# K turned by transposing DMAs from its 16-bit halves, and a part of the up weights split one stage later

## What is computed

```python
h = layernorm(xn, ln_g, ln_b)
q = l2norm(heads(h @ Wq)) * q_scale
k = l2norm(heads(h @ Wk)) * k_scale
logits = where(causal, einsum("bhid,bhjd->bhij", q, k) * 10, -1e9)
out = (softmax(logits) @ heads(h @ Wv)) @ Wo
h = layernorm(out, ln_g, ln_b)
gate = softmax(h @ gate_w + gate_b)
hid = gelu(einsum("bsd,edf->bsef", h, w1) + b1)
moe = sum over e of gate[e] * (hid[e] @ w2[e] + b2[e])
ffn = layernorm(moe, ln_g, ln_b)
```

## Time and profile before

| what | value |
|---|---|
| median of 3 runs | 1125.51 us (1121.51 to 1126.7) |
| the profiled execution's own time | 1120.17 us |
| its span, first to last instruction | 1118.4 us |
| mean granted clock of TensorE | 0.986 |
| busy: PE, PEld, DVE, ACT, POOL | 96%, 82%, 86%, 70%, 25% |

### The profile page before, as it was taken

The page is one execution under the profiler, slowest core; times in us unless marked ns, Lnnn a source line. Parts: engine busy times, 40 slices in busy tenths (PEclk is TensorE's granted clock), DMA queues, the critical chain, the costliest instruction groups (busy, mean ns, idle before and its releaser), DMA issues.

```text
span 1118.4 us, 27576 instructions
## 1 busy us (share of the span) xinstructions
PE 1075.0 (96%) x10435; PEld 912.2 (82%) x10435; DVE 959.6 (86%) x2543; ACT 778.9 (70%) x1772; POOL 277.7 (25%) x328
## 2 busy tenths in 40 slices
PE   4877999999999999999999999999999999999997
PEld 1664888888888888888888888888888888888897
DVE  8988798898988989898898989889898888988763
ACT  5873948668595876859677594867759587685653
POOL 2340314224031231404123140412403132140200
PEclk9995999999999999999999999999999999999999
DMA  7010000000000000000000000000000000000000
GB/s 210 7 39 10 2 11 7 1 16 1 11 7 11 6 2 16 1 11 6 6 11 2 11 7 11 6 1 16 2 11 6 11 7 6 6 6 1 7 2 10
DMA packets 18722, 14.60 MB, mean 13 GB/s; under 512 B 2408, under 2 KB 16160, under 8 KB 18592
## 3 DMA queue, kind: packets, MB, share of 16 engines
q1 hardware_dynamic: 17680, 12.76, 3.8%
q10 hardware_dynamic: 912, 0.09, 0.1%
HBM read 10.75 MB, written 2.10 MB: 11 GB/s over the span
## 4 chain that ended last, share of the span: by engine, by line
PE 89%; DVE 4%; issue 3%; ACT 2%; POOL 1%; SPq 0%; DMA 0%; POOLq 0%; DVEq 0%; ACTq 0%
PE O L565 19%; PE O L468 14%; PE S L484 5%; PE U L547 5%; PE U L548 5%; PE U L549 5%; PE J L382 5%; PE S L449 4%; PE J L343 4%; PE U L449 4%; PE S L404 4%; PE J L344 3%; PE J L345 3%; PE S L400 3%; PE O L475 2%
## 5 line engine op out<-in xcount | busy, mean ns | idle before, releaser
L777 ACT ACTIVATE hid<-U,b1c 128x256 f32<-128x256 f32 x512 | 200.5, 474 | 174.8 <-PE U L549 174.7
L565 PE MATMUL O<-w2s,hid 128*128 128x128 f32 x2048 | 251.1, 276 | 0.0
L565 PEld LDWEIGHTS O<-w2s,hid 128*128 128x128 f32 x2048 | 238.6, 192 | 2.9
L928 POOL TENSOR_SCALAR_AFFINE_SELECT P<-P 128x512 f32<-128x512 f32 x128 | 85.0, 664 | 618.6 <-ACT P L750 618.5
L468 PEld LDWEIGHTS O<-Vx,P 128*128 128x128 f32 x1536 | 188.0, 192 | 30.2 <-issue 14.3
L468 PE MATMUL O<-Vx,P 128*128 128x66 f32 x1536 | 188.6, 273 | 3.6 <-POOL P L928 2.0
L1198 DVE TENSOR_TENSOR_SCAN st<-aexp,u 128x256 f32<-128x256 f32 x256 | 178.8, 698 | 0.4 <-issue 0.3
L920 POOL TENSOR_TENSOR raw<-raw,nr 128x512 f32<-128x512 f32 x124 | 132.8, 1097 | 134.9 <-DVE nr L1066 134.9
L1208 DVE SCALAR_TENSOR_TENSOR y<-st,bc,y 128x256 f32<-128x256 f32 x240 | 133.5, 556 | 8.5
L547 PE MATMUL U<-h2h,w1h 128*128 128x256 f16 x480 | 130.9, 273 | 0.0
L549 PE MATMUL U<-h2h,w1l 128*128 128x256 f16 x480 | 130.9, 273 | 0.0
(11 more groups left out here) (204 smaller groups left out, 2048.0 us busy)
## 6 DMA issues: line engine op xcount, KB each, us to landing
xin<-in_L_attn_x SPq DMA_DIRECT2D x16, 128.0 KB, 2.1
xres<-in_L_attn_x SPq DMA_DIRECT2D x16, 128.0 KB, 2.3
hid<-in_L_ffn_w SPq DMA_DIRECT2D x2, 1024.0 KB, 6.5
out_dram<-fin SPq DMA_DIRECT2D x16, 128.0 KB, 1.8
raw<-in_L_ffn_Wq SPq DMA_DIRECT2D x1, 512.0 KB, 4.7
raw<-in_L_ffn_Wk SPq DMA_DIRECT2D x1, 512.0 KB, 6.4
raw<-in_L_ffn_Wv SPq DMA_DIRECT2D x1, 512.0 KB, 7.4
wos<-in_L_ffn_Wo SPq DMA_DIRECT2D x1, 512.0 KB, 11.4
```

Of the source, the lines that this page charges most:

```text
L565: last = mm(O[e % 2][:, t * P:(t + 1) * P], hid[:, e % 2, m, t * P:(t + 1) * P], w2s[:, e * FC + m, :], start=(m == 0), stop=(m == FC - 1))
L777: fn(hid[:, e % 2, f % FC, :], U[q % 2][:, m * SEQ:(m + 1) * SEQ], ACT.Gelu_apprx_tanh, bias=b1c[:, f:f + 1], scale=1.0 / WS).then_inc(gel ...
```

## The change

From the second sequence on K is not turned by TensorE. `high` copies K from `raw` in SBUF to `Kh`, and `low` leaves `Kl`, both in 16 bits and not yet turned. SyncE then turns them with transposing DMAs from `Kh` to `KTh` and from `Kl` to `KTl`, each 128x128: per quarter four for the high half, then four for the low half. That makes 32 per sequence and 480 in all. A quarter's four raise `kt_high[q]` or `kt_low[q]`, which TensorE waits for. Q stays as it was, but its turns now take the two banks by turns. The first sequence is handled as before.

The second part: the low halves of the second half of the up weights are made in four pieces of 512 columns in `body(1)`'s heads' stage, not in one piece in `body(0)`'s experts' stage, and one state of the first scan moves from the heads' stage into that stage.

The core of the diff (left out: the new tiles and semaphores, and the helper that names Q's bank):

```diff
+            def turn_keys(s, quarter, low):
+
+                if quarter == 0 and not low:
+                    sp.wait_ge(st_ready, s * NP)
+                if low:
+                    sp.wait_ge(t_lo, s * NL + 2 * quarter + 2)
+                else:
+                    sp.wait_ge(t_hi, s * NL + 2 * quarter + 2)
+                src, dst, done = ((Kl, KTl, kt_low) if low else (Kh, KTh, kt_high))
+                for p in (2 * quarter, 2 * quarter + 1):
+                    for t in range(T):
+                        sp.dma_start_transpose(dst[:, p, t * P:(t + 1) * P], src[:, t, p * P:(p + 1) * P]
+                                               ).then_inc(done[quarter], 16)
...
                 if older:
                     store_out(i - 2)
+                if new:
+                    for quarter in range(NP // 2):
+                        turn_keys(i + 1, quarter, False)
+                        turn_keys(i + 1, quarter, True)
...
             def scores_for_max(s, p):
 
-                pe.wait_ge(t_hi, s * NL + 2 * (p // 2) + 2)
+                if s == 0:
+                    pe.wait_ge(t_hi, 2 * (p // 2) + 2)
+                else:
+                    pe.wait_ge(t_hi, s * NL + 2 * (p // 2) + 1)
+                    pe.wait_ge(kt_high[p // 2], s * KT)
...
+                if p % 2 == 0 and s > 0:
+                    pe.wait_ge(kt_low[p // 2], s * KT)
...
                     if old and k == 9:
+                        if not older:
+                            pe.wait_ge(w1_low, 2 * W1PARTS)
                         expert_up(i - 1, 0)
                 for m in range(NE + 2):
                     if new and m in TURN_AT:
                         turn_qk(i + 1, TURN_AT[m])
-                        turn_qk(i + 1, TURN_AT[m] + 1)
...
-                    if not old and m == NE + 1:
-                        pe.wait_ge(w1_low, W1PARTS + 1)
...
+                elif s > 0:
+                    half, c0 = quarter // 2, quarter % 2 * 2 * P
+                    act.wait_ge(unit, s * NJ + half * 4 + 4)
+                    from_one(act, kt_high[quarter], (s - 1) * KT)
+                    fn(Kh[:, :, p * P:(p + 2) * P], raw[:, 4 * half + 1:4 * half + 4:2, c0:c0 + 2 * P], ACT.Copy
+                       ).then_inc(t_hi, 1)
...
+                elif s > 0:
+                    half, c0 = quarter // 2, quarter % 2 * 2 * P
+                    from_one(dve, kt_low[quarter], (s - 1) * KT)
+                    V.tensor_tensor(Kl[:, :, p * P:(p + 2) * P], raw[:, 4 * half + 1:4 * half + 4:2, c0:c0 + 2 * P],
+                                    Kh[:, :, p * P:(p + 2) * P], ALU.subtract).then_inc(t_lo, 1)
...
+                    if old and not older and 1 <= k < 1 + W1PARTS:
+                        split_w1(1, k - 1, W1PARTS)
...
-                    if not old and 1 <= m <= 6:
-                        scan(i, m + 9)
-                        add_state(i, m + 9)
+                    if not old and 1 <= m <= 7:
+                        scan(i, m + 8)
+                        add_state(i, m + 8)
...
-                    if not old and m == 3:
-                        split_w1(1, 0, 1)
```

More of the change, by code:

```diff
@@ L38 @@
 KC = 5
+KT = 2 * T * 16
 def build(nc, x, a_log, b, c, dt_w, dt_b, conv_w, conv_b, ln_g, ln_b, Wq, Wk, Wv, q_scale, k_scale,
@@ L114, in build @@
         KTl = sb("KTl", [P, NP, SEQ], F16)
+        Kh = sb("Kh", [P, T, HD], F16)
+        Kl = sb("Kl", [P, T, HD], F16)
         Vx = sb("Vx", [P, T, H, VW])
@@ L200, in build @@
          y_tr, e_vec, e_root, xb_done, xy_done) = (sems[n] for n in names)
+        kt_high = [sem(f"kt_high{q}") for q in range(NP // 2)]
+        kt_low = [sem(f"kt_low{q}") for q in range(NP // 2)]
         def tiles(ap):
@@ L252, in y_bank, with turned, turn_bank @@
             return S2[:, 1, 0:SEQ] if s == LAST else O[0][:, 0:SEQ]
+        def turned(s, n):
+            return n + 1 if s == 0 else NL + (s - 1) * (NP // 2) + n // 2 + 1
+        def turn_bank(s, n):
+            return J[n % 2] if s == 0 else J[n // 2 % 2]
         def step_bank(s):
@@ L372, in turn_qk @@
                 pe.wait_ge(unit, s * NJ + half * 4 + kind * 2 + 2)
-                if n < 2 and s > 0:
-                    pe.wait_ge(v_done, s * 2 * T + 3 + n)
+                if s > 0 and n < 4:
+                    pe.wait_ge(v_done, s * 2 * T + 3 + n // 2)
+                elif s > 0:
+                    pe.wait_ge(t_lo, s * NL + n - 3)
                 elif n < 2:
@@ L718, in high @@
                 quarter, kind = divmod(n, 2)
-                act.wait_ge(t_ready, s * NL + n + 1)
                 p = 2 * quarter
                 if kind == 0:
-                    fn(QTh[:, p, :], J[n % 2][:, 0:SEQ], ACT.Copy, scale=wcol[:, p:p + 1])
-                    fn(QTh[:, p + 1, :], J[n % 2][:, SEQ:2 * SEQ], ACT.Copy, scale=wcol[:, p + 1:p + 2]
+                    act.wait_ge(t_ready, turned(s, n))
+                    bank = turn_bank(s, n)
+                    fn(QTh[:, p, :], bank[:, 0:SEQ], ACT.Copy, scale=wcol[:, p:p + 1])
+                    fn(QTh[:, p + 1, :], bank[:, SEQ:2 * SEQ], ACT.Copy, scale=wcol[:, p + 1:p + 2]
+                       ).then_inc(t_hi, 1)
[4 more added lines that the diff above has]
+                    fn(Kh[:, :, p * P:(p + 2) * P], raw[:, 4 * half + 1:4 * half + 4:2, c0:c0 + 2 * P], ACT.Copy
                        ).then_inc(t_hi, 1)
                 else:
+                    act.wait_ge(t_ready, turned(s, n))
                     fn(KTh[:, p:p + 2, :].rearrange("p a q -> p (a q)"), J[n % 2][:, :], ACT.Copy).then_inc(t_hi, 1)
```

10 lines of the change are left out of this document (6 added, 4 removed).

## The result

The changed kernel takes **1284.3 us** (median of 4 runs, 1281.01 to 1287.45) against 1123.85 (1121.51 to 1126.7) of the kernel before, measured beside it: a ratio of 1.1426, 95% interval 1.1397 to 1.1455. It is 14% slower; the prediction said 1113.3 us, with a range from 1097 to 1140. The profiled execution has a span of 1284.4 us.

The account below looks back on a forecast made before the run. TensorE was taken to bound 14 of 15 bodies: 25.8 us of removed turns, less 14.7 of waits, plus 1.1 in the first body, gives 12.2 us gained, so 1113.3 us from 1125.5; range 1097 to 1140 us.

Parts of the forecast that it names:

- d: On SyncE's queue, the distance from one transposing DMA issue to the next, taken as 0.51 us.
- the slow rival: SyncE's queue is the bound: TensorE waits at the first, then the seventh pair's scores; 1134 us at d = 1.0; chance 0.27.
- L: Time from a transposing DMA's issue to its landing, taken as 2.1 us from ordinary loads and stores.
- 3d + L - 2.58: TensorE's wait at the first pair's scores for four transposes, forecast at 1.05 us per body, 14.7 us over 14.
- The cover: Time from the end of ScalarE's first K copy to the first pair's scores, hiding 2.58 us of the transposes.
- The removed turns: K's turns leaving TensorE, worth 1.84 us per sequence, 25.8 us over the 14 bodies that TensorE bounds.
- The first body: First sequence's body, where VectorE sets the pace: moving the split gains 1.1 us (0 to 2.2), K's turns nothing.
- The split's pieces: Four 0.57 us pieces in body 1's heads' stage, hidden in VectorE's 8.2 us of idle time; otherwise costing 2.3 us once.
- The later quarters: Transposes after the first quarter: a group takes 2 us, scores come 9.1 us or more later, so nobody waits.
- The copies from SBUF: ScalarE's copy of K and VectorE's subtraction, now with SBUF as source, taken as unchanged in time.
- The clock: TensorE at the lower clock, 1.2 GHz, behind long waits, said to make them cost some more, without a figure.
- What would show it wrong: First-pair wait over 1.8 us or near nothing, waits at third, fifth or seventh pair, or TensorE's clock falling in middle bodies.

## Why the prediction was wrong

**The step that failed** is the choice of d, the distance from one transposing issue to the next: "I take d = 0.51, the slowest unhindered issue, because a turn asks at least as much of its issuer as a copy". It measured 1.27 us. "At least as much" is a lower bound, and I used it as the value; the only upper end in the text, d = 1.8, is a store's landing and no row of a transposing DMA, and the text said that above d = 1.0 each 0.1 us costs 38 us. The chance of that rival, 0.27, was too low for a quantity that no row showed.

- **The mechanism was right, as the slow rival.** Its place (the first pair's scores, then the seventh's, through SyncE's queue) is what the trace shows, and its formula with d = 1.27 and L = 2.4 gives 3d + L - 2.58 = 3.63 us for the first wait (measured 3.38) and 27 x 1.27 + 2.4 - 26.8 = 9.9 for a body, hence 1125.5 + 14 x (9.9 - 1.84) - 1.1 = 1237 us. The other 47 us are smaller steps. A body lost 10.65 us where the formula has 9.9 - 1.84 = 8.05, which is 36 us over 14: the issues are uneven (24 of them took 31.66 us, 1.32 each), which puts the seventh pair 1.7 us later, and the clock behind its wait adds 1.7 us in the long bodies. And the first body, which the prediction left out of the queue's count, lost 12 us where 1.1 gained had been counted.
- **The landing** was near: L = 2.1 taken, 2.4 measured.
- **The cover** of the first wait was 2.84 us and not 2.58 (from the copy's end at 611.92 to 618.14 - 3.38 = 614.76): with the turns worth less, TensorE came to the scores later. That is why the first wait is 3.38 and not 3.63.
- **The Trainium skill's number** ("VectorE: DVE Perf Modes", section "The three transpose paths", 1309 ns for a 128x128 block by DMA) agrees with the distance measured here, 1.27 us, not with the landing of 2.4. The prediction had worked it out as distance and landing both, 1237 us; that the two measured values give the same time is chance, since 27 distances that are 0.04 us too long make up for a landing that is 1.09 too short. It is not a price of the block, though: 128x512 cost SyncE the same.
- **The removed turns** were sized at 1.84 us a body and gave 1.37 of TensorE's time. I halved a group of eight; a group of four takes 0.44 to 0.56, not 0.435 to 0.485, and the matmuls between two groups got 0.11 us longer.
- **The first body**: 1.1 us forecast, 2.4 measured with the split alone, just past the upper end of 2.2. In the changed kernel the queue swamped it (62.59 to 74.38 us); "K's turns gain nothing in this body" was right, but they could lose there, and I did not say so.
- **The split's pieces** in body 1's heads' stage are hidden, as said: in the run with the split alone they lie between 107 and 118 us, and TensorE is busy for 31.69 of 31.69 us of that stage (101.42 to 133.11).
- **The later quarters** "are covered" followed from d alone, and fell with it: waits stood at the fifth and the seventh pair, in some bodies at the third.
- **The copies from SBUF** taken as unchanged: 0.64 us on ScalarE against 0.61, and on VectorE 0.78 against 0.68 on average, all of it beside GpSimd's work.
- **The clock**: named only as "some more". In the changed kernel it fell to 1.2 GHz behind the first pair's wait in 13 of 14 bodies (the four matmuls took 0.50 us, and 0.34 in the other one).
- **What would show it wrong** named the three signs that came: a wait over 1.8 us, waits at the fifth and seventh pair, the clock in the middle bodies.

With two issues per quarter in place of four the wait is 0.93 us, close to the 1.05 of the forecast, and the kernel is 6.1 us faster, half of the 12.2 forecast. The form of the sum holds for a kernel in which the queue is not the bound. That its wait comes out is luck: one distance of 1.27 us and a landing of 2.4 make 3.67 us, and the forecast had three of 0.51 and 2.1, 3.63. Of the rest, the removed turns at 1.37 in place of 1.84 us take 6.6 us off.

**Not tried.** A second engine issuing half of the transposes would test whether the 1.27 us belong to SyncE or to the transposing path. The Trainium skill ("DMA: Bandwidth & Descriptors", section "DMA Transpose (X-bar)") says that two descriptor streams that transpose at once can silently corrupt each other's output; no run here shows it. The question stays open. Open too is why the clock falls behind some waits of 3.4 us and not behind others.

## What to carry to other kernels

Count transposing DMAs before their bytes: one cost 1.27 to 1.42 us of its issuing queue whatever its shape from 64x128 to 128x512, so many small blocks in series became the bound where a few wide ones fitted under other work. Where a term of the sum has no row, do not take the lower bound as its value, and look at what the far end would do to the sign. And of a chain of transfers, compare when the last one that is needed lands with when it is needed; what waits first is not what costs most.

## What the runs showed that I had not expected

- The issue of a transposing DMA takes 1.27 to 1.42 us of SyncE's queue for 64x128 as for 128x512, more than twice an ordinary one (0.37 to 0.51 in the earlier trace rows, 0.58 for a load of x in the changed kernel), with a landing hardly longer (2.4 us against 1.8 to 2.3 in the earlier trace rows).
- Thirty-two such DMAs per sequence beside a busy TensorE cost nothing measurable (ratio 0.9998), as long as nobody waits.
- A wait of 3.4 us could put TensorE at 1.2 GHz for 9 us more, so that 50 us of repeated matmuls in the place of such waits made the kernel 15 us faster.
- VectorE's subtraction with both inputs in SBUF took up to 1.50 us beside a working GpSimd and 0.68 without; moving it to GpSimd left VectorE busier than it was (982.7 us against 973.8).
